# Four fused transformer layers on one core: early expert tiles planned a stage earlier, and turned one tile ahead

## The reference, cut to what matters

```python
# layer 0: a shared pair of experts for every token, and 8 routed experts (grouped), hidden 128
out = shared.at[flat_idx].add(routed_out)
# layer 1: 8 experts with hidden size 512, the two best of each token, weighed by a softmax
weights_BSK, indices_BSK = jax.lax.top_k(probs_BSE, TOP_K)
act_BSEF = jax.nn.silu(gating_BSEF)
fuse_BSEF = act_BSEF * up_BSEF
down_BSED = jnp.einsum('BSEF,EFD->BSED', fuse_BSEF, kernel_down_EFD)
out_BSD = jnp.einsum('BSED,BSE->BSD', down_BSED, full_weights_BSE)
```

## Time and profile before

| what | value |
|---|---|
| median of 3 runs | 1650.57 us (1648.32 to 1651.87) |
| the profiled execution, its own time | 1650.38 us |
| its span, first to last instruction | 1648.6 us |
| granted TensorE clock, mean share of full speed | 0.88 |
| TensorE busy | 1313.9 us (80%) |
| TensorE weight loads busy | 1075.4 us (65%) |
| VectorE busy | 827.0 us (50%) |
| ScalarE busy | 443.7 us (27%) |
| last row of `phase1`'s last turn (the router logits) | ends near 474.6 us |
| early tiles | 485 to 655 us |
| expert loop of layer 1, from its first turned rows | 658.45 us on |

### The profile page before, as it was taken

One profiled execution on the slowest core, in us unless ns is written; L12 is line 12 of the kernel. 1 busy time (PEld: TensorE's weight loads), 2 busy tenths in 40 slices (PEclk: granted clock), 3 DMA queues, 4 the chain that ended last, 5 costly groups with the idle time before them and its releaser, 6 DMA issues. The chain is left out here.

```text
span 1648.6 us, 25825 instructions
## 1 busy us (share of the span) xinstructions
PE 1313.9 (80%) x8174; PEld 1075.4 (65%) x8186; DVE 827.0 (50%) x2325; ACT 443.7 (27%) x1122; POOL 286.5 (17%) x307
## 2 busy tenths in 40 slices
PE   5876486596569887999977877777359999999997
PEld 3553353453347676888855655555359999999996
DVE  2249768868866766212246666665622222222222
ACT  2636235235222322111223232322101111111111
POOL 2010021020020002000233343442311111111111
PEclk9788777677769998999979889888679999999999
DMA  9993041041074477888400011010168888889884
GB/s 339 351 291 99 1 144 57 0 157 44 23 249 167 140 250 245 284 295 300 147 10 29 19 33 40 28 38 1 43 256 318 318 314 310 311 319 326 311 315 152
DMA packets 116317, 291.51 MB, mean 177 GB/s; under 512 B 8192, under 2 KB 90528, under 8 KB 101024
## 3 DMA queue, kind: packets, MB, share of 16 engines
q1 hardware_dynamic: 106032, 273.00, 47.1%
q0 software_dynamic: 10224, 17.77, 4.2%
HBM read 218.84 MB, written 71.90 MB: 176 GB/s over the span
## 5 line engine op out<-in xcount | busy, mean ns | idle before, releaser
L810 PE MATMUL bank<-norm_cols,work 128*128 128x128 f32 x3744 | 469.2, 281 | 29.2 <-DMA work<-in_moe 12.5
L810 PEld LDWEIGHTS bank<-norm_cols,work 128*128 128x128 f32 x3744 | 457.6, 197 | 45.7 <-issue 29.6
L1715 DVE TENSOR_TENSOR extra<-bank,span 128x256 f32<-128x256 f32 x202 | 85.4, 424 | 389.9 <-ACT span L1510 389.9
L810 PE MATMUL bank<-work,extra 128*128 128x256 f32 x808 | 206.9, 380 | 0.0
L1510 ACT ACTIVATE span<-bank 128x256 f32<-128x256 f32 x202 | 77.4, 383 | 449.9 <-PE bank L810 449.9
L810 PEld LDWEIGHTS bank<-work,extra 128*128 128x128 f32 x808 | 138.6, 191 | 10.7
L2924 POOL DMA_INDIRECT out_x<-att_rows,slot_token x39 | 60.7, 1556 | 377.7 <-ACT att_rows L1520 313.6
L2743 POOL TENSOR_TENSOR rstd<-var_eps,neg_half 128x4 f32<-128x4 f32 x18 | 18.3, 1018 | 521.9 <-DVE var_eps L1727 521.9
L810 PE MATMUL bank<-weights,norm_cols 128*128 128x512 f32 (+1 forms) x192 | 89.3, 615 | 8.3 <-ACT norm_cols L1541 5.5
L810 PE MATMUL bank<-work 128*128 128x256 f32 (+4 forms) x260 | 63.3, 383 | 27.7 <-ACT work L1541 12.3
L909 PE MATMUL bank<-ident,work 128*128 128x128 f32 x256 | 53.0, 366 | 36.3 <-DVE att_rows L1715 27.2
(11 more groups left out here) (349 smaller groups left out, 1976.9 us busy)
## 6 DMA issues: line engine op xcount, KB each, us to landing
work<-in_moe SPq DMA_DIRECT2D x78, 1024.0 KB, 7.5
work<-in_moe SPq DMA_DIRECT2D x39, 2048.0 KB, 7.8
expert_rows_in<-zero SPq DMA_DIRECT2D x3, 5590.0 KB, 47.2
expert_rows_in<-zero SPq DMA_DIRECT2D x3, 5504.0 KB, 35.9
expert_rows_out<-zero SPq DMA_DIRECT2D x3, 5504.0 KB, 22.4
work<-in_moe SPq DMA_DIRECT2D x31, 512.0 KB, 5.7
att_cols<-expert_rows_in SPq DMA_DIRECT2D x39, 130.0 KB, 2.0
att_cols<-expert_rows_in SPq DMA_DIRECT2D x39, 128.0 KB, 3.5
```

Source lines behind the costliest of these rows:

```text
L810: return pe.matmul(o, l, r, start=a, stop=z)
L1715: return dve.tensor_tensor(o, a, b, op)
```

## The change

`plan_early` is split into `plan_early_counts` and `plan_early_tiles`. Both run in the last turn of `phase1` on VectorE, behind the four gates; the adds of y 0 and y 1 stand between them and those of y 2 and y 3 behind. For this VectorE's loop has two turns, and its third turn is written out straight. On SyncE the up and down weights of tile 0 are loaded as soon as the plan is there and the attention outputs `xo` are done, into the first 2048 columns of `WREG` and into `V0`; then come the wait for the scatters, the rows of tiles 0 and 1, the wait for the last down product, and the weights of tile 1. Even tiles now use these new buffers. The four third-phase loads that go to the first columns of `WREG` are issued behind the store of tile 15. The transposes of a tile are a function of their own (`early_turn`, and `early_turned` on ScalarE), and stand between the up products of the tile before and the down products of the one before that; the rows of tile j+4 are loaded behind the transposes of tile j+2.

```diff
-        MROWF = V0[0:1, :, :, :].rearrange("p t h n -> p (t h n)")
+        MROWF = SPAN[0:1, :, :].rearrange("p h k -> p (h k)")
-               "early": [BIG[:, 6592:8640], BIG[:, 9664:11712]]}
+               "early": [WREG[:, 0:2048], BIG[:, 6592:8640]]}
-               "early": [BIG[:, 8640:9664], XN[:, :, :].rearrange("p t n -> p (t n)")]}
+               "early": [V0[:, 0:2, :, :].rearrange("p t h n -> p (t h n)"), BIG[:, 8640:9664]]}
...
-                sp.wait_ge(sem("rows_sent"), 16 * 2 * T * last)
-                sp.sem_inc(sem("norm_rows_free"), 1)
...
                     sp.wait_ge(sem("early_planned"), 1)
+                    filled(jf, GROUPS - 2, ("xo", T - 1))
+                    early_up(0)
+                    early_down(0)
+                    sp.wait_ge(sem("rows_sent"), 16 * 2 * T * (GROUPS - 1))
+                    sp.sem_inc(sem("norm_rows_free"), 1)
+                    early_rows(0)
+                    early_rows(1)
                     filled(jf, GROUPS - 2, ("acc", "y", T - 1))
-                    for j in range(2):
-                        early_rows(j)
-                        early_up(j)
-                        early_down(j)
+                    early_up(1)
+                    early_down(1)
+                    sp.wait_ge(sem("results_zeroed"), 16 * yrows.shape[0])
+                    filled(jg, 0, ("ex", 0))
+                    early_rows(2)
                     for j in range(-1, EARLY - 2):
                         if j + 3 < EARLY:
-                            filled(jg, 0, ("ex", j + 1))
-                            early_rows(j + 3)
                             filled(jg, 0, ("eu", j + 1, h - 1))
                             early_up(j + 3)
+                        if j + 4 < EARLY:
+                            filled(jg, 0, ("ex", j + 2))
+                            early_rows(j + 4)
...
                     early_store(EARLY - 1)
+                    load_third_phase(None)
...
-                for dst, src in w3loads[3 * share:3 * share + 3]:
+                for dst, src in w3loads[0:4] if share is None else w3loads[4 + 3 * share:7 + 3 * share]:
...
-            sp.wait_ge(sem("results_zeroed"), 16 * yrows.shape[0])
...
@@ tensor: early_up loses its transposes, which become
+            def early_turn(j):
+                u = j % 2
                 pe.wait_ge(sem(f"rows_loaded{u}"), 16 * (j // 2 + 1))
                 ps, b = fill(jg, 0, ("ex", j))
                 for c in range(KC):
                     last = pe.transpose(ps[:, c * P:(c + 1) * P], XS[:, u, c * P:(c + 1) * P], ident[:, :])
                 last.then_inc(bank_full[b], 1)
...
                 for j in EARLY_AT[where]:
                     if j + 1 < EARLY:
                         early_up(j + 1)
+                    if j + 2 < EARLY:
+                        early_turn(j + 2)
                     early_down(j)
...
+            early_turn(0)
             early_up(0)
+            early_turn(1)
             early_tiles("opening")
@@ scalar: the copy into xsT moves in the same way (early_turned)
...
@@ vector
-                    if i > 1:
+                    if i > 1 and not last_turn:
                         add_y(i - 2)
+                if last_turn:
+                    plan_early_counts()
+                    add_y(0)
+                    add_y(1)
+                    plan_early_tiles()
                 add_y(T - 2)
                 add_y(T - 1)
...
-                plan_early()
...
-            with dve.Fori(0, GROUPS - 1) as n:
+            with dve.Fori(0, GROUPS - 2) as n:
                 enter(n, STEPS["phase1"])
                 phase1(jf, n, n + 1, n)
-            leave(GROUPS - 1)
+            leave(GROUPS - 2)
+            straight(lambda: phase1(jf, GROUPS - 2, GROUPS - 1, GROUPS - 2, True))
```

## The result

The changed kernel took **1637.2 us** (median of five runs, 1632.64 to 1639.62) against 1650.57 before: ratio 0.9912, 95% interval 0.9891 to 0.9933, or 13.4 us less. Run again beside the experiments it gave 1638.35 twice; all 17 executions have a median of 1637.8. The forecast was 1641.5 (1637.5 to 1648). The sign was right, the gain was 13.4 us and not 9.2, and the time lies just under the range. The profiled execution took 1637.2 us.

The account below looks back on a forecast made before the run. TensorE was taken to set the pace, with holes from waits in the gap. Gains of 5.2 and 5.5 less 1.5 gave 9.2 us off 1650.4, plus 0.3 for bubbles: 1641.5 us, range 1637.5 to 1648.

Parts of the forecast that it names:

- Part 1: VectorE's last feed-forward turn: early tiles planned there, plan ending at 474.7 against 481.9, 7.2 us earlier.
- Part 2: Tile 0's loads at the gap's opening: first up products at 484.3 instead of 489.51, 5.2 us gained, bounds 2.7 and 6.9.
- SyncE's wait for it ended at 478.2: SyncE's wait for the last scatter, taken from the old trace; tile 0's rows then go out at 479.3.
- the bound on the rows' landing: Tile 0's rows land 2.0 to 6.2 us after issue, said to cover scatters and rows delayed by weights.
- rival B: Opening: scatter, not plan, releases tile 0's rows, landing at 485.5; only 2.7 us gained there, 1649.7 overall; chance 0.1.
- Part 3: Early tiles in the gap: turning ahead removes copy waits, 0.5 us a tile, 5.5 us in all, bounds 2.5 and 7.
- So tiles 11 to 13 give nothing beyond what VectorE inherits.: List stage: VectorE paces and reaches tile 10's gates without idle time, so these tiles gain nothing of their own.
- Tile 5: Its second half's 3.79 us wait for VectorE stays and grows; earlier gains are kept, its own is lost.
- rival A: Gap: only the opening gains, as waits for gates or weights replace the copy waits; 1646.7 us, chance 0.15.
- Part 4: Head of the expert stage: four moved 256 KB loads delay rows and weights, costing 1.5 us, bounds 0 and 5.
- The sign that I had named: A wait of 1 to 3 us for rows or weights near the expert loop's third tile.
- Part 5: VectorE's last turn written straight: taken as 0, between up to 1 us gained and 3.6 us lost.

Follow-up runs that it names:

- ahead only: The kernel before with nothing but the tiles turned ahead, rows loaded accordingly; run twice: 1635.65 us (ratio 0.9907) and 1639.81 us (0.9922).
- turned late: The changed kernel with each tile's transposes back at the head of its own up products; 1649.83 us, ratio 0.9984.

## Why the prediction was right in sign and short in size

**What bounds the kernel.** Right: TensorE and its holes in the gap. The one-part kernels add up there: 9.6 to 10.1 (ahead only) and 3.2 (turned late) make 12.8 to 13.3 of the gap's 13.7.

**Part 1, the planning.** Right to 0.3 us in each row: plan, down products, router logits, weights' issue.

**Part 2, the opening: 5.2 us forecast, 3.8 measured.** The failed term is "SyncE's wait for it ended at 478.2". I took that wait over from a trace in which nothing else was in flight and then put 1.5 MB in flight ahead of the wait's end. It ended at 481.7. The rows then landed in 2.0 us and not 3.7, which gave 1.7 of the 3.3 back. The Trainium skill ("DMA: Bandwidth & Descriptors", the section on queues, rings and completion order) has the rule, that an engine shares itself packet by packet between its queues. The prediction cited it, and named the scatters, but gave it no term in the sum and left it to the bound on the rows' landing. The bound did hold (2.7 to 6.9 us, 3.8 measured); the sum's 478.2 did not. The kernel with its rows first shows it (2.45 against 6.1 us). The early request for weights is worth nothing. So rival B had half of it: the scatters and not the plan do release the rows, but at 481.7 and not so late that the gain was lost.

**Part 3, tiles turned ahead: 5.5 us forecast, 9.6 to 10.1 measured.** This is the step that made the forecast miss. Two terms of it failed.
- "so the wait (0.56 at 529.58) goes; the transposes stay. I take 0.5 us a tile". Each tile gained 0.8: 0.75 at tile 2, and 4.5 from the second half of tile 5 to tile 10, where 2.5 was forecast. From transposes to the first product stood 1.0 us, 0.56 to 0.62 of it idle. What remains of it is 0.22, because the next products follow into the array at once. The other 0.2 was shown as busy, and is gone where other products follow; I read it as the end of the transposes' way through the array. The Trainium skill ("TensorE: Matmul & The Clock Gate", back-to-back overlap in the step-by-step section) says that the drain of one product overlaps the fill of the next, and the rows agree: 0.38 us of transposes take 0.22 of the engine's time.
- "So tiles 11 to 13 give nothing beyond what VectorE inherits." They gave 2.9 us (6.6 to 9.5). I took one VectorE row without idle time ahead of it for a stage in which VectorE paces. Copy waits of 1.05 and 2.17 us at tiles 11 and 12 were on the path, with ScalarE late, and only then did a new wait for gates (2.48) take a part back. TensorE before the change, tiles 10 to 13:

```profile
600.44 3.81 PE L810 MATMUL bank<-norm_cols,work 128*128 128x128 f32 x32 [0.62 <-ACT norm_cols L1458]
...
610.15 5.23 PE L810 MATMUL bank<-norm_cols,work 128*128 128x128 f32 x32 [1.05 <-ACT norm_cols L1458]
...
619.77 5.44 PE L810 MATMUL bank<-norm_cols,work 128*128 128x128 f32 x32 [2.17 <-ACT norm_cols L1458]
...
627.78 3.81 PE L810 MATMUL bank<-norm_cols,work 128*128 128x128 f32 x32 [0.62 <-ACT norm_cols L1458]
```

A part of the 2.9 us came through the clock, which the sum had at nothing. Behind the wait of 2.17 us tile 12's products ran at a granted clock of 0.68 (619.7 to 625.0 us) and took 5.3 us; in the changed kernel they ran at 1.00 (2.4 GHz, 606.3 to 612.7) and took 3.9 beside their wait. Tile 11's took about 0.5 us longer than before, at 0.69 against 0.70, so some 0.9 us is left. Why the clock stayed up at tile 12 no run shows.

Tile 5 went as forecast: its wait stayed and grew from 3.79 to 4.76, and its own gain was lost. Tiles 14 and 15 gave 0.8, not 1.8, since a new wait of 1.7 us for VectorE's normalized rows stands ahead of tile 14, and the loop's rows took 0.7 back. These moved waits have the form of rival A, whose bet was that all gains would end so; of the 11.1 us of copy waits that went they put back 5.1 (1.0 at tile 5, 2.5 at tile 12, 1.7 ahead of tile 14).

**Part 4, the loads: 1.5 us forecast, about 1.8 found,** as a difference of means that the stage's own variation nearly covers. The sign that I had named did not come: of the 1 to 3 us of waiting near the third tile the profiled execution shows 0.36 for rows, and 0.76 for weights, a wait that the kernel before had too, with the same 0.76 (at 672.23).

**Part 5, straight code: 0 forecast, 0 measured.**

**Sum.** 3.8 + 9.6 to 10.1 - 1.8 is 11.6 to 12.1 us, against 13.4 measured with an interval of 11.1 to 18.0. Between the medians some 1.5 us isn't located; the stages behind, which the change doesn't touch, vary by more. Between the two profiled executions all 13.2 us are: 0.1 ahead of the gap, 13.7 in it, 1.4 lost in the expert stage, 0.8 gained behind. Because of this the whole change and turning ahead alone can't be told apart by time: medians of all executions are 1637.8 (17) and 1637.8 (10). By the traces the early plan adds 3.8 us in the gap and pays about 1.8 in the expert stage; that its 2 us are there is argued from the stages, not shown by a time.

**The range.** The parts' own bounds gave 13.9 us at best, 1636.5; I drew the lower end 1.0 above that, because ends rarely meet. Part 3 alone went 2.6 to 3.1 us past its bound of 7, and part 2's shortfall of 1.4 hid some of it. The median of all 17 executions, 1637.8, would lie just inside the range, by that luck; it makes neither term right.

## What to carry to other kernels

A wait of TensorE for a copy between transposes and products costs more than its idle time: count from the start of the transposes to the start of the products and take off what they need when others follow at once. When a transfer is asked for earlier, price every transfer that completes behind it, also those of another queue on which the wait stands, here the scatters. When a wait moves, look at the granted clock behind it too: it was 0.50 behind the 4.8 us of waiting at tile 5 (543.3 to 547.0 us) and 1.00 behind the 2.5 us at tile 12 (610.8 to 612.7). One row without idle time doesn't make an engine the bound of a stage; look whether the engine fed by it has waits for somebody else there.

## What the runs showed of the hardware

- A 128 KB scatter that was complete 2.45 us behind its issue, with nothing but scatters in flight, took 6.1 us with 1.5 MB of direct loads behind it in time but on another queue, and 5.7 with 1 MB.
- The third phase, same code, took 409.7 us in one execution of the changed kernel and 404.7 in another, with TensorE busy 287.9 and 283.9 us:

```profile
788.80:1198.50 409.70, 287.90 (x1338) 218.06 (x1337) 239.82 (x740) 107.81 (x271) 155.70 (x160) 0.83 0.12 39
```

```profile
786.10:1190.80 404.70, 283.93 (x1338) 215.34 (x1336) 239.42 (x739) 107.37 (x271) 155.40 (x160) 0.84 0.12 40
```

  The granted clock differs by 0.01 there. Of the changed kernel's 17 executions the three shortest (1629.5, 1629.7, 1632.6 us) had a mean clock of 0.882 or 0.883, the others 0.870 to 0.878 but for one at 0.884. A gain of 2 us needs the stage's own length to be seen; six executions don't show it.
- In the hole of 8 us ahead of tile 0 the granted clock falls (0.50 from 484 to 486 us), which is the lower level of 1.2 GHz, and the 32 products take 5.95 us where later ones take 3.8. Neither the change nor any variant whose opening is shown here got rid of this: each left TensorE idle there for over 8 us, in one piece or two.
